# Causal scores packed into 11 PSUM banks per unit instead of 16, cards dealt by bank, and the middle turns as a straight program

## The chip, the cores and the metric

One Trainium2 chip, one core of it. The metric is device microseconds of one execution, the median of several runs. TensorE (PE in the profile) does the matrix products, PEld is its loading of weights, VectorE is DVE, ScalarE is ACT, GpSimd is POOL, and SyncE (SP) issues most transfers. Each engine runs its own program in order and waits on semaphores.

## The reference

Two layers over `x` of shape (8, 512, 256) with a context of shape (8, 512, 128). What matters here is the attention; H = 16 heads of D = 16.

```python
# layer 0
att  = einsum('bhqd,bhkd->bhqk', q, k) * scale            # self attention over 512 tokens
att  = where(causal, att, -inf)
y    = einsum('bhqk,bhkd->bhqd', softmax(att), v)
attc = einsum('bhqd,bhkd->bhqk', qc, kc) * scale          # cross attention with the context
y    = y + einsum('bhqk,bhkd->bhqd', softmax(attc), vc)
x    = x + y @ Wp + bp
x    = x + ffn_with_ternary_weights(layernorm(x))         # 256 -> 1024 -> 256, GELU
# layer 1
x    = x + cross_attention(layernorm(x), ctx) @ Wo + bo   # no mask
x    = x + ffn_with_one_scale_per_tensor(layernorm(x))    # 256 -> 1024 -> 256, GELU
```

## The kernel before, in words

**Units.** The attention is cut into 96 units: 8 batches, three kinds of attention (`x` cross of layer 0, `s` causal self of layer 0, `f` cross of layer 1) and four groups of HU = 4 heads. A *turn* of the program holds 12 units in the order x0 to x3 and s0 to s3 of batch b, then f0 to f3 of batch b - 1. One name, such as s1, stands for the unit of that kind and group in the turn under discussion. `ORDER` is the whole list.

**A unit.** q and k are split into three bf16 parts each, so a product of 96 rows has nearly the precision of f32; these rows lie in a `stack` tile (ring of four), loaded from memory by SP. The unit's work has two halves that are done in different units of time:

- *maxima*: for each tile of 128 queries and each head PE writes scores into a bank of the ring `mx` (2 banks), and DVE reduces each bank to its negated row maxima (`nmax`). Units x and f have 16 banks of 512 columns. Units s already have 11 (`MX_CAUSAL`): the masked part is not computed, so tile 0 of all four heads (4 x 128 columns) shares a bank, tile 1 (256 columns) has two heads in a bank.
- *scores*: POOL splits `nmax` in three bf16 parts (`negmax`), PE turns them (`negmax_T`), ACT copies them to `nrow` and issues a small transfer of 12 KB that writes them as three more rows of the stack. PE then forms the transposed scores, keys on the partitions, with the maximum subtracted, tile j of keys and head c at a time, into a bank of the ring `st` (3 banks); ACT takes the exponential into `probs` (2 slots, one per j); PE multiplies them by the values into `acc` (`values`), ACT copies `acc` to `heads`, PE turns that and DVE divides by the row sums (`heads_out`).

In units s the scores of tile j are 512 - 128 j columns wide: 512, 384, 256 and 128. Before the change each (j, c) has a bank of its own: 16 banks and 16 exponentials. In the diagonal block a product of the identity with a 128 x 128 mask (`mask_st`, `mask_mx`) is added behind each head's product.

**Order.** `unit_slot` writes out the order of a unit's steps. It has 16 *places*, one for each (j, c). At each place stand the scores of that bank; then some banks of the maxima of the unit after next (`third`), dealt evenly by `deal`; at the last place of tile j the `values` of tile j - 1, and at the last place of tile 0 the `values` of the last tile of the unit before with the copy of its `acc`. `negmax` of the next unit stands at place 2, `negmax_T` of the next unit at place 8, which is (j, c) = (2, 0). The transfer that loads the stack of the unit after the next two (`fourth`) is at the unit's beginning. Last come the *cards*, the other work (projections, layer norms, the feed-forward net, residuals), which `slots` deals evenly over the places of several units; `None` is an empty card that keeps a distance.

In a middle turn the cards are: 89 over x0 to s0 (end of layer 1 two batches back, feed-forward net and start of layer 1 of the batch before, the last 17 being the projections fk0, fk1, fq0, fq1 with `settle`, on which the stacks of f0 to f3 depend), 9 over s1 (tokens of the next batch: `load_mid`, `ctx_T`, `stats`, `norm`, `norm_T`), 19 over s2 and s3 (`v` and projections of the next batch's x), 6 and more over f0, and the blend of `ffn_norm` with the projections of the next batch's s over f1 to f3. I write s0.12 for place 12 of unit s0.

**Program.** `walk` writes out turns 0 and 1, then a hardware loop (`eng.Fori`) with five passes for the turns 2 to 6, then turn 7 and the rest. Each engine has its own copy of that loop, so it is left and begun again four times on each. In the loop the semaphores' values are computed from the loop's register (`Count.at`).

The line that ties the loop to 16 places is the choice of bank, `st[n.times(HU * NT).slot(ST_BANKS, k)]`.

Of the kernel before, what the change touches and what calls it, by code (L numbers as in the profile page):

```python
# [36 lines left out]
P = 128  # L37
# [7 lines left out]
HU = 4  # L45
# [36 lines left out]

def exists(u, last):

    return u[0] + (u[1] == "f") <= last


def neighbour(u, k, last=B):

    n = AT[u] + k  # L90
    return ORDER[n] if 0 <= n < len(ORDER) and exists(ORDER[n], last) else None

# [22 lines left out]
def unit_slot(u, others, last, first=False):  # L115
# [10 lines left out]
    for j in range(NT):  # L126
        for c in range(HU):
            out.append(("scores", u, j, c))
            out += maxima[HU * j + c]
            if c == 3 and j:  # L130
                out.append(("values", u, j - 1))
            if (j, c) == (0, 3) and prev:
                out += [("values", prev, NT - 1), ("heads_copy", prev)]
            if (j, c) == (1, 1) and prev:
                out.append(("heads_out", prev))
            if (j, c) == (0, 2) and next_:
                out.append(("negmax", next_))
            if (j, c) == (2, 0) and next_:
                out.append(("negmax_T", next_))
            out += others[HU * j + c]  # L140
# [3 lines left out]
def slots(units, others, last, first=False):  # L144

    out, places = [], NT * HU
    others = deal(others, places * len(units))
    for k, u in enumerate(units):
        out += unit_slot(u, others[places * k:places * k + places], last, first and k == 0)
    return out  # L150
# [141 lines left out]

class Count:
# [23 lines left out]
class Step:  # L317
# [12 lines left out]

    def mx(self, later=0):
# [5 lines left out]
def walk(eng, steps_of):  # L337

    def walk_turn(keys, i):
# [11 lines left out]
def two_layers_kernel(nc, x, ctx_512, L0_xattn_Wk, L0_xattn_bk, L0_xattn_Wq, L0_xattn_bq, L0_xattn_Wv, L0_xattn_bv,  # L351
# [4 lines left out]
    with ExitStack() as ctx:  # L356
# [238 lines left out]
        def st_bank(n, k):  # L595

            return st[n.times(HU * NT).slot(ST_BANKS, k)]
# [5 lines left out]
        def _(sp):  # L603
# [64 lines left out]
            def stack_(s):  # L668
                r, p, g = s.n.slot(STACKS), s.unit[1], s.unit[2]
                if s.n.base >= STACKS:  # L670
                    sp.wait_ge(exp_done, s.n.times(16, ST_BANKS - 16 * (STACKS - 1)).at())
# [214 lines left out]
        def _(act):  # L886
# [38 lines left out]
            def scores(s):  # L925
                (j, c), n = s.args, s.n
                w = T - P * j if s.unit[1] == "s" else T
                if c == 0:
                    act.wait_ge(values_done, n.times(4, VD - P_SLOTS + j + 1).at())
# [599 lines left out]
```

## Time and profile before

| | |
|---|---|
| median of 3 runs | 2048.04 us (2047.91 to 2049.11) |
| profiled execution, its own time | 2049.73 us |
| its span in the trace | 2047.9 us |
| PE / PEld busy | 1735.0 us (85%) / 745.0 us (36%) |
| DVE / ACT / POOL busy | 1348.7 (66%) / 1168.0 (57%) / 739.7 us (36%) |
| mean granted clock of TensorE | 0.911 |

How to read it: PE's busy time counts each matmul from its start to a modelled end, and the matmuls overlap; the time that PE really takes for one is the distance from its start to the start of the next. The granted clock is 1.00 at 2.4 GHz and 0.50 at 1.2 GHz. "Idle before" in a row is time in which the engine did nothing, and behind the arrow stands what ended it; "issue" means that no awaited work is visible.

### The profile page before, as it was taken

What the parts mean: (1) busy time and instruction counts of PE and PEld (TensorE: products, weight loads), DVE (VectorE), ACT (ScalarE), POOL (GpSimd) and SP (SyncE); (2) the same over time, 40 slices, a digit from 0 to 9 for tenths busy, and PEclk for the clock granted to TensorE, in tenths of its full rate; (3) what the DMA queues carried; (4) which work ended last, traced back from release to release, by engine and by line L of the source; (5) the groups of instructions that cost most, each with busy time, mean ns of one, the idle gap of its engine ahead of it and who ended that gap; (6) DMA issues with size and microseconds to landing.
All of it is one profiled execution on the core that took longest, in us unless ns stands there. A gap on an engine that the chain in (4) does not pass through costs nothing.

```text
span 2047.9 us, 34236 instructions
## 1 busy us (share of the span) xinstructions
PE 1735.0 (85%) x10004; PEld 745.0 (36%) x10016; DVE 1348.7 (66%) x2478; ACT 1168.0 (57%) x2178; POOL 739.7 (36%) x984
## 2 busy tenths in 40 slices
PE   5897889987999889987999799987999798777676
PEld 1243334422443244432543244332442243231225
DVE  6567666777667666757677756766677757617378
ACT  1364475566655485556655585557555675552486
POOL 3322525541544126521544136521544042150034
PEclk7798889998999989987999999988999899786898
DMA  7224313232232313331232313222331223005023
GB/s 204 81 77 122 83 32 89 78 90 62 64 104 59 94 48 85 87 81 52 68 100 70 83 48 102 74 77 59 90 87 55 65 56 101 1 26 161 23 81 103
DMA packets 106988, 159.93 MB, mean 78 GB/s; under 512 B 20657, under 2 KB 83249, under 8 KB 106801
## 3 DMA queue, kind: packets, MB, share of 16 engines
q1 hardware_dynamic: 101904, 156.43, 27.7%
q8 instruction: 96, 1.57, 0.3%
q10 hardware_dynamic: 4896, 1.18, 0.3%
q14 instruction: 92, 0.75, 0.1%
HBM read 105.00 MB, written 51.38 MB: 76 GB/s over the span
## 4 chain that ended last, share of the span: by engine, by line
PE 56%; DVE 14%; issue 11%; ACT 8%; POOL 7%; DMA 2%; SPq 1%; ACTq 1%; DVEq 0%; POOLq 0%
PE acc L1390 13%; PE mx L1355 12%; PE st L1376 10%; DVE nmax L1176 8%; PE misc L1330 6%; PE misc L1302 3%; PE misc L1342 3%; PE misc L1417 3%; ACT probs L931 2%; PE misc L1444 2%; POOL qk L823 1%; DMA stack<-parts_fk 1%; POOL parts L825 1%; POOL parts L821 1%; POOL parts L827 1%
## 5 line engine op out<-in xcount | busy, mean ns | idle before, releaser
L1176 DVE TENSOR_REDUCE nmax<-mx 128x1 f32<-128x512 f32 (+2 forms) x1376 | 881.4, 674 | 458.0 <-PE mx L1355 276.7
L931 ACT ACTIVATE probs<-st 128x512 f32<-128x512 f32 (+3 forms) x1536 | 773.7, 548 | 516.1 <-PE st L1376 346.4
L1355 PE MATMUL mx<-stack 96*128 96x512 bf16 (+3 forms) x1536 | 574.3, 385 | 128.7 <-DVE nmax L1176 80.6
L1376 PE MATMUL st<-stack 99*128 99x512 bf16 (+3 forms) x1536 | 565.8, 378 | 68.6 <-ACT probs L931 57.6
L1376 PEld LDWEIGHTS st<-stack 99*128 99x128 bf16 x1536 | 152.0, 100 | 443.9 <-ACT probs L931 262.2
L1355 PEld LDWEIGHTS mx<-stack 96*128 96x128 bf16 x1536 | 154.6, 101 | 342.9 <-DVE nmax L1176 237.4
L821 POOL TENSOR_TENSOR parts<-qk,zero 128x512 bf16<-128x512 f32 x94 | 98.1, 1043 | 302.5 <-ACT qk L914 302.5
L833 POOL TENSOR_TENSOR nparts<-nmax,zero 128x16 bf16<-128x16 f32 x96 | 21.1, 220 | 405.4 <-DVE nmax L1176 398.2
L1390 PE MATMUL acc<-probs,v_x 128*32 128x512 f32 x1024 | 151.0, 665 | 0.0
L1390 PE MATMUL acc<-probs,v_f 128*32 128x512 f32 x1024 | 147.4, 650 | 0.4 <-ACT probs L931 0.3
L1379 PE MATMUL st<-mask_st,identb 128*128 128x128 bf16 x512 | 112.2, 222 | 0.0
L827 POOL TENSOR_TENSOR parts<-qk,parts 128x512 bf16<-128x512 f32 x94 | 108.9, 1158 | 7.4
L823 POOL TENSOR_TENSOR qk<-qk,parts 128x512 f32<-128x512 f32 x94 | 108.7, 1157 | 7.4
L1358 PE MATMUL mx<-mask_mx,identb 128*128 128x128 bf16 x512 | 101.9, 224 | 0.0
L825 POOL TENSOR_TENSOR parts<-qk,zero 128x512 bf16<-128x512 f32 x94 | 97.9, 1042 | 7.4
L1390 PE MATMUL acc<-probs,v_s 128*32 128x512 f32 (+3 forms) x1024 | 97.6, 454 | 0.0
L1330 PE MATMUL misc<-xnT_A,W 128*128 128x512 f32 x192 | 93.2, 608 | 0.0
L859 POOL TENSOR_TENSOR hq<-hid,magic 128x1024 bf16<-128x1024 f32 x32 | 60.6, 1893 | 81.8 <-ACT hid L966 81.8
L938 ACT COPY heads<-acc 128x512 f32<-128x512 f32 x96 | 56.3, 586 | 50.5 <-PE acc L1390 50.3
L890 ACT COPY nrow<-misc 48x128 bf16<-48x128 bf16 x96 | 24.2, 252 | 94.5 <-PE misc L1365 93.7
L1379 PEld LDWEIGHTS st<-mask_st,identb 128*128 128x128 bf16 x512 | 51.1, 100 | 38.2 <-issue 22.3
L1302 PE MATMUL misc<-ident,heads 128*128 128x128 f32 x384 | 61.7, 284 | 3.5 <-ACT heads L938 3.2
(231 smaller groups left out, 2051.5 us busy)
## 6 DMA issues: line engine op xcount, KB each, us to landing
parts_xk<-parts SPq DMA_DIRECT2D x48, 128.0 KB
parts_xq<-parts SPq DMA_DIRECT2D x48, 128.0 KB
stack<-parts_xq SPq DMA_DIRECT2D x32, 192.0 KB, 3.1
stack<-parts_xk SPq DMA_DIRECT2D x32, 192.0 KB, 3.7
parts_sk<-parts SPq DMA_DIRECT2D x48, 128.0 KB
parts_sq<-parts SPq DMA_DIRECT2D x48, 128.0 KB
stack<-parts_sq SPq DMA_DIRECT2D x32, 192.0 KB, 2.9
stack<-parts_sk SPq DMA_DIRECT2D x32, 192.0 KB, 3.5
```

What stands on the lines that cost most here:

```text
L821: pool.tensor_tensor(part[0], qk[:, r, :], zero[:, :].to_broadcast([P, T]), ALU.add).then_inc(qk_split[r], 1)
L823: pool.tensor_tensor(qk[:, r, :], qk[:, r, :], part[0], ALU.subtract).then_inc(qk_split[r], 1)
L825: pool.tensor_tensor(part[1], qk[:, r, :], zero[:, :].to_broadcast([P, T]), ALU.add).then_inc(qk_split[r], 1)
L827: pool.tensor_tensor(part[2], qk[:, r, :], part[1], ALU.subtract).then_inc(qk_split[r], 1)
L931: act.activation(probs[:, j % P_SLOTS, c, T - w:], st_bank(n, 4 * j + c)[:, 0:w], ACT.Exp, scale=SCALE).then_inc(exp_done, 1)
L1176: dve.tensor_reduce(nmax[:, ring, first:first + NT * (len(cs) - 1) + 1:NT], src, AX.X, ALU.max, negate=True).then_inc(mx_free, 1)
L1302: last = pe.transpose(o[:, P * m:P * m + P], t_, id_[:, :])
L1330: last = pe.matmul(misc[misc_slot(s)][:, :], W[w][:, k, P * m:P * m + P], src[:, k, :], start=k == 0, stop=k == ks - 1)
L1355: last = pe.matmul(o, stack[0:ROWS, r, 0, c, P * i:P * i + P], stack[0:ROWS, r, 1, c, 0:w], start=True, stop=not causal)
L1376: last = pe.matmul(o[:, 0:w], stack[0:AUG, r, 1, c, P * j:P * j + P], stack[0:AUG, r, 0, c, T - w:T], start=True, stop=not causal)
L1379: last = pe.matmul(o[:, 0:P], identb[:, :], mask_st[:, :], start=False, stop=True)
L1390: last = pe.matmul(acc[32 * c:32 * c + 32, T - w:T], v_aug[p][:, j, HU * g + c, :], probs[:, j % P_SLOTS, c, T - w:T], start=j == 0, stop= ...
```

## The change

- `ST_CAUSAL` gives the scores of a causal unit 11 banks: tiles 0 and 1 four banks each of one head, tile 2 two banks of two heads (2 x 256 columns), tile 3 one bank of four heads (4 x 128). PE fills a bank with one wait and one signal, ACT takes it with one exponential.
- Where a head's share of the bank is exactly 128 columns (tile 3 of the scores, tile 0 of the maxima), the mask is written first, as one product 512 columns wide whose moving operand repeats the 128 columns of the mask four times; the heads' products are added to it.
- A causal unit has 11 places instead of 16, and maxima and cards are dealt over those. So x0 to s0 have 75 places instead of 80, s1 11 instead of 16, and s2 with s3 22 instead of 32. `negmax_T` moves to place 8 of 11, which is again the first bank of tile 2.
- The hardware loop is gone: all turns are written out, and all semaphore values are constants. The bank ring's position is counted by `ST_BEFORE`.

```diff
+ST_FULL = [(j, [c], T) for j in range(NT) for c in range(HU)]
+ST_CAUSAL = [(j, [c], T - P * j) for j in (0, 1) for c in range(HU)] + [(2, [c, c + 1], 2 * P) for c in (0, 2)] + \
+    [(3, [0, 1, 2, 3], P)]
...
 def unit_slot(u, others, last, first=False):
-    maxima = deal([("maxima", third, k) for k in banks_of(third)] if third else [], NT * HU)
+    banks = scores_in(u)
+    maxima = deal([("maxima", third, k) for k in banks_of(third)] if third else [], len(banks))
...
+    for k, (j, cs, w) in enumerate(banks):
+        nth = k - min(m for m, bank in enumerate(banks) if bank[0] == j)
+        ends = k == last_of_tile(u, j)
+        out.append(("scores", u, k))
+        out += maxima[k]
+        if ends and j:
+            out.append(("values", u, j - 1))
+        if ends and j == 0 and prev:
+            out += [("values", prev, NT - 1), ("heads_copy", prev)]
+        if (j, nth) == (1, 1) and prev:
+            out.append(("heads_out", prev))
+        if (j, nth) == (0, 2) and next_:
+            out.append(("negmax", next_))
+        if (j, nth) == (2, 0) and next_:
+            out.append(("negmax_T", next_))
+        out += others[k]
...
 def walk(eng, steps_of):
-    walk_turn(TURNS[0], None)
-    with eng.Fori(0, B - 3) as i:
-        walk_turn(TURNS[1], i)
-    walk_turn(TURNS[-1], None)
+    for keys in TURNS:
         for key in keys:
             if key[0] in steps_of:
-                steps_of[key[0]](Step(key, i))
+                steps_of[key[0]](Step(key, None))
...
             def scores(s):      # ACT
-                act.wait_ge(st_full, n.times(16, 4 * j + c + 1).at())
-                act.activation(probs[:, j % P_SLOTS, c, T - w:], st_bank(n, 4 * j + c)[:, 0:w], ACT.Exp, scale=SCALE).then_inc(exp_done, 1)
+                act.wait_ge(st_full, n.at(k + 1))
+                act.activation(probs[:, j % P_SLOTS, cs[0]:cs[-1] + 1, T - w:],
+                               st_bank(n, k)[:, 0:len(cs) * w].rearrange("p (c w) -> p c w", w=w),
+                               ACT.Exp, scale=SCALE).then_inc(exp_done, 1)
...
             def scores(s):      # PE; maxima in the same manner
-                last = pe.matmul(o[:, 0:w], stack[0:AUG, r, 1, c, P * j:P * j + P], stack[0:AUG, r, 0, c, T - w:T],
-                                 start=True, stop=not causal)
-                if causal:
-                    last = pe.matmul(o[:, 0:P], identb[:, :], mask_st[:, :], start=False, stop=True)
+                whole = causal and w == P
+                if whole:
+                    pe.matmul(o[:, :], identb[:, :], mask_st[:, :].unsqueeze(1).to_broadcast([P, len(cs), P]), start=True, stop=False)
+                for c in cs:
+                    own = o[:, (c - cs[0]) * w:(c - cs[0]) * w + w]
+                    last = pe.matmul(own, stack[0:AUG, r, 1, c, P * j:P * j + P], stack[0:AUG, r, 0, c, T - w:T],
+                                     start=not whole, stop=c == cs[-1] if whole else not causal)
+                    if causal and not whole:
+                        last = pe.matmul(own[:, 0:P], identb[:, :], mask_st[:, :], start=False, stop=True)
```

## Rows read from the trace of the kernel before

**Rows 1.** The page: busy time of each engine
```profile
PE 1735.0 (85%) x10004; PEld 745.0 (36%) x10016; DVE 1348.7 (66%) x2478; ACT 1168.0 (57%) x2178; POOL 739.7 (36%) x984
```

**Rows 2.** Windows of turns 2, 3, 6, f3's copy to next; busy, clock, DMA
```profile
454.74:682.25 227.51, 201.13 (x1188) 86.28 (x1188) 152.97 (x294) 134.76 (x262) 87.47 (x118) 0.95 0.29 78
682.25:910.92 228.67, 202.58 (x1188) 86.38 (x1188) 153.13 (x294) 134.56 (x262) 87.48 (x118) 0.94 0.28 76
...
1368.06:1592.64 224.58, 201.00 (x1188) 86.45 (x1188) 152.83 (x294) 134.54 (x262) 87.51 (x118) 0.95 0.28 75
```

**Rows 3.** Timeline of PE where turn 4 begins
```profile
902.35 1.07 PE L1390 MATMUL acc<-probs,v_f 128*32 128x512 f32 x8
905.77 0.39 PE L1376 MATMUL st<-stack 99*128 99x512 bf16 x1 [2.35 <-issue]
```

**Rows 4.** Waits: engine line, waited for; us in total, times, longest
```profile
PE st L1376 <- issue: 10.6, 4, 3.0
PE mx L1355 <- DMA stack<-parts_fk: 26.4, 8, 9.0
```

**Rows 5.** Timeline of PE at s2.0 of turns 3 and 4
```profile
797.00 0.39 PE L1355 MATMUL mx<-stack 96*128 96x512 bf16 x1 [2.57 <-DMA stack<-parts_fk]
...
1027.80 0.39 PE L1355 MATMUL mx<-stack 96*128 96x512 bf16 x1 [2.17 <-DMA stack<-parts_fk]
```

**Rows 6.** Windows, copy of s0's acc to that of s1's, turns 3 and 4
```profile
783.70:803.08 19.38, 15.86 (x117) 9.28 (x116) 12.68 (x31) 8.56 (x23) 5.64 (x13) 0.91 0.58 148
1014.92:1032.20 17.28, 14.17 (x117) 8.14 (x116) 12.59 (x31) 8.57 (x23) 5.66 (x13) 1.00 0.62 164
```

**Rows 7.** Timelines of POOL and SP: fk0's first split, loading f0's stack
```profile
767.11 1.04 POOL L821 TENSOR_TENSOR parts<-qk,zero 128x512 bf16<-128x512 f32 x1 [5.08 <-ACT qk L914]
...
792.10 1.35 SPq L678 DMA_DIRECT2D stack<-parts_fk  x3
```

**Rows 8.** Windows, acc copy to acc copy, of x2, x3, s0 and s2, turn 3
```profile
731.66:750.38 18.72, 16.22 (x134) 8.40 (x133) 8.96 (x18) 16.20 (x26) 8.39 (x8) 1.00 0.28 65
750.38:768.18 17.80, 17.58 (x129) 9.61 (x128) 12.27 (x30) 12.09 (x24) 4.68 (x4) 1.00 0.20 46
768.18:783.70 15.52, 14.82 (x113) 7.51 (x112) 7.25 (x13) 8.53 (x22) 14.52 (x17) 1.00 0.18 56
...
803.08:818.65 15.57, 14.97 (x94) 6.30 (x93) 10.85 (x19) 8.49 (x21) 9.89 (x13) 1.00 0.11 32
```

**Rows 9.** Timelines of PE and ACT from negmax_T in s0 of turn 7
```profile
1698.28 0.22 PE L1365 MATMUL misc<-identb,nparts 128*48 128x128 bf16 x1 [0.61 <-POOL nparts L839]
1698.88 0.73 ACTq L922 DMA_DIRECT2D stack<-nrow  x1
...
1702.74 0.39 PE L1376 MATMUL st<-stack 99*128 99x512 bf16 x1
```

**Rows 10.** DMA issues: KB each, median us from issue to landing
```profile
stack<-parts_xk SPq DMA_DIRECT2D x32, 64.0 KB, 3.7
x_later<-y_s SPq DMA_DIRECT2D x1, 512.0 KB, 2.6
```

**Rows 11.** Timeline of PE in s2's last tile
```profile
811.18 0.22 PE L1376 MATMUL st<-stack 99*128 99x128 bf16 x1
811.24 0.22 PE L1379 MATMUL st<-mask_st,identb 128*128 128x128 bf16 x1
811.30 0.38 PE L1355 MATMUL mx<-stack 96*128 96x512 bf16 x1
811.52 0.22 PE L1376 MATMUL st<-stack 99*128 99x128 bf16 x1
```

**Rows 12.** Groups by line and shape: busy us, mean ns of one, idle before
```profile
L1176 DVE TENSOR_REDUCE nmax<-mx 128x1 f32<-128x512 f32 x1152 | 749.9, 686 | 324.0 <-PE mx L1355 276.7 <-PE mx L1358 39.5 <-POOL nparts L837 1.8
L931 ACT ACTIVATE probs<-st 128x512 f32<-128x512 f32 x1152 | 642.2, 602 | 429.9 <-PE st L1376 346.4 <-PE st L1379 78.0 <-ACT nrow L890 1.6
L931 ACT ACTIVATE probs<-st 128x128 f32<-128x128 f32 x128 | 31.1, 278 | 26.3 <-PE st L1379 25.0
```

More of the change, by code:

```diff
@@ L91, in neighbour, with scores_in, last_of_tile @@
     return ORDER[n] if 0 <= n < len(ORDER) and exists(ORDER[n], last) else None
+def scores_in(u):
+    return ST_CAUSAL if u[1] == "s" else ST_FULL
+def last_of_tile(u, j):
+    return max(k for k, bank in enumerate(scores_in(u)) if bank[0] == j)
 def banks_in(u):
@@ L122, in unit_slot @@
     next_, third, fourth = (neighbour(u, k, last) for k in (1, 2, 3))
-    maxima = deal([("maxima", third, k) for k in banks_of(third)] if third else [], NT * HU)
+    banks = scores_in(u)
+    maxima = deal([("maxima", third, k) for k in banks_of(third)] if third else [], len(banks))
     if fourth:
         out.append(("stack", fourth))
[L126 to L140, printed above, removed]
+    for k, (j, cs, w) in enumerate(banks):
[14 more added lines that the diff above has]
+        out += others[k]
     return out
 def slots(units, others, last, first=False):
-    out, places = [], NT * HU
-    others = deal(others, places * len(units))
+    out, places = [], [len(scores_in(u)) for u in units]
+    others = deal(others, sum(places))
     for k, u in enumerate(units):
-        out += unit_slot(u, others[places * k:places * k + places], last, first and k == 0)
+        done = sum(places[:k])
+        out += unit_slot(u, others[done:done + places[k]], last, first and k == 0)
     return out
@@ L290 @@
     MX_BEFORE.append(MX_BEFORE[-1] + len(banks_in(u)))
+ST_BEFORE = [0]
+for u in ORDER:
+    ST_BEFORE.append(ST_BEFORE[-1] + len(scores_in(u)))
 class Count:
@@ L329, in ring, with st @@
         return Count(START[key or self.key][r], RING_PER_TURN[r], self.i)
+    def st(self, later=0):
+        return Count(ST_BEFORE[AT[self.unit] + later], 0, None)
     def mx(self, later=0):
@@ L595, in st_bank @@
         def st_bank(n, k):
-            return st[n.times(HU * NT).slot(ST_BANKS, k)]
+            return st[n.slot(ST_BANKS, k)]
         block = ctx.enter_context(nc.Block())
@@ L670, in stack_ @@
                 if s.n.base >= STACKS:
-                    sp.wait_ge(exp_done, s.n.times(16, ST_BANKS - 16 * (STACKS - 1)).at())
+                    sp.wait_ge(exp_done, s.st(1 - STACKS).at(ST_BANKS))
                 for w, name in enumerate("qk"):
@@ L1387, in values @@
                     pe.wait_ge(heads_full, n.at(1))
-                pe.wait_ge(exp_done, n.times(16, 4 * j + 4 + ST_BANKS).at())
+                pe.wait_ge(exp_done, s.st().at(last_of_tile(s.unit, j) + 1 + ST_BANKS))
                 for c in range(HU):
```

35 lines of the change are left out of this document (19 added, 16 removed).

## The prediction

> **What bounds the kernel now.** I read the page first, then the windows turn by turn and unit by unit, then the waits, then the timelines at the places they named. PE is busy 85% of the span, DVE 66%, ACT 57%, POOL 36% [rows 1]. The windows of single units show what that average hides: in x3 and s0 PE is busy 17.58 of 17.80 and 14.82 of 15.52 us, so these units last as long as PE's instructions. In x2 it is busy 16.22 of 18.72, and ACT with 16.20 is as loaded as PE [rows 8]. In s2 DVE has 10.85 of 15.57 us, ACT 8.49: ACT bounds no causal unit.
>
> So the question for each part is which of PE's instructions or idle times it changes. Two idle times stand out.
>
> First, the loop's ends. PE's first scores of turn 4 come 2.35 us after the modelled end of its last work, and the releaser is "issue" [rows 3]. The list of waits has exactly four of these at that line, 10.6 us in all [rows 4], and the loop of five passes starts anew four times. The turns show what one costs with all that hangs on it. Turn 3 lasts 228.67 us, and turns 4 and 5 repeat it within 0.3; each begins behind a restart and has one in its last unit. Turn 6, after which the loop is only left, has none in its last unit and lasts 224.58: 4.1 us less. Turn 2 has one at its end but is entered, not restarted: 227.51, 1.15 us less [rows 2]. This second part I read as what a stall leaves behind it, mainly a slower clock.
>
> Second, at s2.0 PE starts the maxima of f0 and waits for f0's stack, 2.57 us in turn 3 and 2.17 in turn 4 [rows 5]; eight such waits make 26.4 us, the longest of 9.0 in the last part, which the change leaves alone [rows 4]. That leaves 17.4 us in turns 1 to 7. It costs more than the wait: s1's window lasts 19.38 us in turn 3 at a clock of 0.91, and 17.28 in turn 4 at 1.00 [rows 6]. Less the 0.40 by which the waits differ, 1.7 us are the clock. I found 0.91 in five of the seven turns.
>
> **The change part by part.**
>
> *No loop.* It removes four restarts at 4.1 + 1.15 = 5.25 us: 21.0 us. Turns 0, 1 and 7 are straight program already and show no wait of this kind (four in all, all at restarts), so nothing is expected in its place. For waits on constants instead of computed values I give nothing: inside the loop too PE's products follow each other at 0.06 and 0.22 us [rows 11], which is their streaming. On what a restart costs, the Trainium skill has two rules. "Runtime: NRT & Kernel Launch", in "Instruction fetch mechanics", says that a taken branch to a page outside the small window makes the engine fetch before it goes on; the idle time of 2.35 us agrees in kind. "Advanced Engine Details and Errata", in "Control Flow Timing", gives a compare-and-branch 108 ns: by that alone, an estimate, four restarts were worth 0.4 us and the term of 21.0 would be gone.
>
> *Fewer exponentials.* Two heads of tile 2 and all four of tile 3 share one. For tile 3 ACT saves 4 x 278 - 602 = 510 ns [rows 12], some 0.8 us in a unit with tile 2, 27 us over 32 units. All of it lies under PE's work (ACT is idle for 7 us in s2) and brings nothing; without that cover it would bring those 27.
>
> *Wide masks.* PE takes 0.06 us from one product of 128 columns to the next, and 0.22 for 512 columns [rows 11]. Before, four heads cost 8 x 0.06 = 0.48 us; after, 0.22 + 4 x 0.06 = 0.46. Columns set the time, not the number of products. Two such banks in 32 units: 0 to -2.6 us; I take 0. That a repeated operand is read slower no row shows; bound: the mask as dear as four separate ones, +1 us.
>
> *Cards by bank, x0 to s0.* 89 cards on 75 places in place of 80. Card 72 (counting from 0), fk0, falls on place 75 x 73 / 89, that is x3.13; before it was s0.1. It gains four places of x3 and s0, at (17.80 + 15.52) / 32 = 1.04 us each [rows 8]; without their share of cards I take 3.2 us. fk0's split begins at 767.11, f0's stack is issued until 793.45, PE goes on at 797.00 [rows 5, 7]: a chain of 29.9 us that POOL and SP set, while PE reaches the place after 27.3. With 3.2 more, PE arrives after 30.5, later than the stack. fq1 moves from s0.12 to s0.7 and remains ahead of POOL. So the waits vanish, but for a rest of the longest: 16.8 of the 17.4. Since the distance ends only 0.6 us on the good side, I take 15; bounds 8 and 17. The slow clock after them: 5 x 1.7 = 8.5, of which I take 7; bounds 0 and 9.
>
> *The same, feed-forward net.* Its steps stand 6% closer together. x2 gains `down_T` and `down` of the third tile, s0 loses projections. Work moves from units that PE fills into one that ACT nearly fills [rows 8]. PE's time is the same; its waits for ACT and POOL in x0 to x2 may grow by the distance lost, up to 1 us a turn. I take +2 in all; bounds -3 and +7.
>
> *Maxima in s2 and s3.* 16 banks on 11 places instead of 16: one or two at a place. DVE needs 16 x 0.686 = 11.0 us for them [rows 12] and PE has only two banks. Before, tile 3 was the tight spot (0.34 us of PE for each place [rows 11] against 0.69 of DVE); after, tiles 0 and 1 are, with 11 maxima, while tiles 2 and 3 have 5. Both orders lose about 1.2 us a unit by my count: 0, bounds -8 and +8 over 16 units.
>
> *negmax_T nearer to the next unit.* This is the new wait. In turn 7's s0 PE takes 4.46 us from negmax_T to the next unit's first scores [rows 9], with seven score places, five banks of maxima and 0.5 of waiting for DVE on the way. After the change two places (384 columns or 0.16 us less) and two banks of maxima (3 x 0.27 less) are left: 4.46 - 0.16 - 0.8 - 0.5 = 3.0, and I take 2.9 for s0, 3.0 for s3; with the norm's transposes in between 3.75 in s1, with a projection 3.95 in s2. In that time ACT must copy and the transfer must land, and all later PE work is queued behind that wait, DVE and ACT behind PE. The issue comes 0.60 us after negmax_T; landing is not shown. Above: in turn 7 scores began 3.86 us after the issue, without idle time before them [rows 9], so at most 3.86. Below: nothing is issued faster than its own 0.73. Rows beside it: 64 KB into the stack land after 3.7, the fastest row after 2.6 [rows 10]. With so small a transfer I take 2.6: the chain is 3.2, and waits are 0.3 in s0 and 0.2 in s3, 0.5 x 8 turns = +4 us. At 3.86 the chain is 4.46, waits 1.6, 1.5, 0.7, 0.5, 4.3 a turn: +34. At best 0. "DMA: Bandwidth & Descriptors", section "Anatomy of one DMA — SWDGE (gpsimd) path", in the Trainium skill has a fixed cost of about 2.0 us; as an estimate from it the chain is 2.6 us and this term 0.
>
> **Sum.** -21 - 15 - 7 + 2 + 0 + 4 = -37 us. Against the profiled execution's 2049.7 us (span 2047.9, 1.8 around it) that is 2012.7; its own time is 1.7 above the median, so against 2048.0 it is **2011 us**, 1.8% less.
>
> **Rivals.**
>
> *A: only the loop pays.* f0's stack is late all the same, because the chain starts when PE reaches fk0, and denser cards delay PE before it. For: the new slack is 0.6 us only. Against: s0 has fewer cards ahead of s1. Then -21 + 2 + 4 = -15: 2033.
>
> *B: slower.* The transfer of `nrow` at the end of each causal unit takes the place of the waits removed. The other terms are -41 together, 5.1 us a turn. With a chain of t us the waits are (t - 2.9) + (t - 3.0) + (t - 3.75) + (t - 3.95), which is 5.1 at t = 4.7, a landing of 4.1 us. At t = 5.0 it is 6.4 a turn, +51: 2058. For: in s1 the DMA engines are 58% busy and move 148 GB/s [rows 6], and 64 KB took 3.7. Against: 3.86 sufficed in turn 7.
>
> *C: the restart is cheap* and the four idle times belong to the turn's first step. Then 21 less gain: 2032. Against: the entry and the exit of the loop carry the same step without it. The 108 ns that the Trainium skill gives for a branch would mean this.
>
> *D: better still.* Sparser maxima and free DVE take the 8 us, negmax_T costs nothing, 17 and 9 are full: 2048 - 21 - 17 - 9 - 8 - 3 = 1990.
>
> **Chances and range.** Forecast 0.64, A 0.16, B 0.08 (half of it slower than before), C 0.04, D 0.08. The range of 1994 to 2034 leaves out D's end, B and a part of A: the low end is the sum with -17, -9, -3, no negmax wait and half of the 8; the high end is A, or the forecast with a landing of 3.3 us. About 0.2% (4 us) is what a measurement tells from no change: faster by more 0.91, within 0.03, slower by more 0.06.
>
> **What would show it.** No "issue" waits of PE at the scores; turns 2 to 6 alike, at 217 to 220 us where they were 228. At s2.0 no wait for stack<-parts_fk above 1 us in turns 1 to 6 and clock 1.00 in s1; else the step of four places is wrong. Idle time before the first scores of s1 and f0 below 0.5 us; above 1.5, B. Exponentials 32 x 5 fewer with s units no shorter for it. What would make the forecast wrong most: a landing above 3.2 us, or a POOL that reaches fk0 late.

## The result and the profile after

The changed kernel takes 2037.16 us (median of 4 runs, 2036.70 to 2038.55), the kernel before beside it 2048.57 us (4 runs): a ratio of 0.9943 with a 95% interval of 0.9925 to 0.9960. It is faster, by 11.4 us and not by the 37 us forecast: the direction was right, the size was not, and the time lies outside the range of 1994 to 2034. The profiled run has a span of 2035.1 us where it was 2047.9.

The page's first lines, after; the counts of PE's products and ACT's exponentials fell as computed, busy times hardly [rows 1]:

```profile
span 2035.1 us, 28512 instructions
...
PE 1716.1 (84%) x9812; PEld 722.3 (35%) x9824; DVE 1343.8 (66%) x2478; ACT 1154.5 (57%) x2018; POOL 742.2 (36%) x984
```

The list of PE's waits, after:

```profile
PE mx L1382 <- DVE nmax L1199: 107.3, 155, 5.3
...
PE mx L1382 <- DMA stack<-parts_fk: 17.8, 5, 9.0
...
PE st L1408 <- DMA stack<-nrow: 4.1, 5, 1.1
```

The four waits for "issue" at the scores [rows 4] are gone. The wait for the first feed-forward net's stack fell from 26.4 to 17.8 us. The wait for `nrow` came at the size expected. The first line is the one that the prediction never asked for. In the trace of before it reads:

```profile
PE mx L1355 <- DVE nmax L1176: 80.6, 122, 5.1
```

PE waits 26.7 us more for DVE's maxima, in 33 more places. The windows (start to end, length, then busy time of PE, PEld, DVE, ACT and POOL, clock, DMA share, GB/s) say where the time went. After, turns 2, 3 and 6, then x0, x2, x3, s0, s1 (also of turn 4), s2 and s3 of turn 3, and s1 of turn 0:

```profile
465.77:689.54 223.77, 200.58 (x1164) 83.41 (x1164) 151.99 (x294) 133.16 (x243) 87.62 (x118) 0.94 0.29 77
689.54:911.75 222.21, 198.19 (x1164) 83.35 (x1164) 152.14 (x294) 132.93 (x242) 87.62 (x118) 0.95 0.28 77
1355.17:1577.21 222.04, 197.20 (x1164) 83.15 (x1164) 151.87 (x294) 133.04 (x242) 87.62 (x118) 0.96 0.29 77
...
689.54:716.92 27.38, 22.19 (x103) 8.96 (x103) 19.08 (x39) 10.73 (x20) 2.13 (x6) 0.88 0.50 136
...
740.95:760.11 19.16, 17.00 (x142) 9.16 (x141) 9.39 (x17) 15.99 (x27) 8.42 (x12) 1.00 0.24 62
760.11:779.12 19.01, 17.79 (x117) 8.88 (x116) 12.65 (x31) 12.05 (x23) 9.10 (x9) 1.00 0.02 5
779.12:793.50 14.38, 14.38 (x109) 7.26 (x108) 7.30 (x13) 8.15 (x16) 13.36 (x18) 1.00 0.48 139
793.50:808.19 14.69, 12.81 (x102) 7.05 (x101) 11.79 (x31) 7.54 (x16) 2.42 (x8) 1.00 0.64 171
1015.59:1030.77 15.18, 12.95 (x102) 7.01 (x101) 11.73 (x31) 7.62 (x17) 2.49 (x8) 1.00 0.64 166
808.19:824.11 15.92, 14.67 (x91) 6.13 (x92) 10.72 (x19) 8.40 (x17) 10.01 (x10) 1.00 0.12 35
824.11:837.09 12.98, 12.53 (x82) 4.93 (x81) 10.02 (x18) 7.25 (x15) 10.35 (x16) 1.00 0.48 134
...
160.12:188.35 28.23, 15.66 (x102) 6.40 (x101) 15.93 (x23) 8.51 (x15) 2.58 (x7) 0.75 0.47 136
```

A middle turn lasts 222 to 224 us where 217 to 220 was forecast. In turn 3 s1 stands at a clock of 1.00 and at 14.69 us (it was 19.38, [rows 6]), s2 is 0.35 us longer and s3 0.2 shorter, x3 is 1.2 us longer and s0 as much shorter [rows 8]. Two windows are far longer than before. Their rows of before, x0 of turns 2 and 3 and s1 of turn 0, are:

```profile
454.74:477.98 23.24, 19.85 (x101) 8.37 (x101) 18.44 (x38) 10.84 (x21) 2.13 (x6) 1.00 0.58 160
682.25:706.49 24.24, 21.10 (x101) 8.56 (x101) 18.62 (x38) 10.84 (x20) 2.12 (x6) 0.93 0.52 135
...
161.98:181.51 19.53, 13.58 (x112) 6.72 (x111) 13.93 (x21) 8.55 (x21) 2.65 (x10) 0.83 0.58 164
```

x0 takes 27.0 to 27.4 us in every middle turn and in turn 7, where it took 23.2 to 24.3 (26.0 in turn 4); s1 of turn 0 takes 28.2 instead of 19.5. Summed over turns 2 to 6 (acc copy to acc copy, before to after, in us): x0 121.9 to 136.4, x1 126.8 to 121.6, x2 93.6 to 96.1, x3 89.0 to 95.1, s0 77.6 to 71.7, s1 94.1 to 75.6, s2 and s3 143.9 to 144.4, f0 to f2 291.8 to 286.9, f3 99.3 to 83.6. Turns 0 and 1 together are 11 us longer.

The timelines of DVE and PE in x0 of turn 3 show why. Before, DVE:

```profile
694.41 1.89 DVE L1176 TENSOR_REDUCE nmax<-mx 128x1 f32<-128x512 f32 x3
696.22 1.37 DVE L1093 TENSOR_SCALAR xn_C<-x,mv_E,rstd_E 128x256 f32<-128x256 f32 x4
```

After, DVE:

```profile
700.54 1.40 DVE L1104 BATCH_NORM_STATS2 stats_E<-x 128x6 f32<-128x256 f32 x4
701.85 0.41 DVE L1108 BATCH_NORM_AGGREGATE mv_E<-stats_E 128x2 f32<-128x6 f32 x4
702.18 1.26 DVE L1199 TENSOR_REDUCE nmax<-mx 128x1 f32<-128x512 f32 x2
703.85 1.38 DVE L1116 TENSOR_SCALAR xn_C<-x,mv_E,rstd_E 128x256 f32<-128x256 f32 x4 [0.41 <-POOL rstd_E L805]
```

and PE, which needs the banks that DVE empties behind that:

```profile
702.90 0.39 PE L1382 MATMUL mx<-stack 96*128 96x512 bf16 x1 [0.51 <-DVE nmax L1199]
...
705.89 0.39 PE L1382 MATMUL mx<-stack 96*128 96x512 bf16 x1 [1.78 <-DVE nmax L1199]
...
707.81 0.61 PE L1382 MATMUL mx<-stack 96*128 96x512 bf16 x1 [1.31 <-DVE nmax L1199]
```

Between the statistics and the norm stood three sets of maxima before (one set is DVE's reduction of one bank) and stand two now: by the denser dealing `norm` and `finish` moved from places x0.12 and x0.13 to x0.11 and x0.12, while `stats` stayed at x0.9. So DVE reaches the norm before POOL has `rstd` and waits 0.41 us, and what follows is all on DVE, four norms, 1.38 us together, and a peak of 1.2, with fewer maxima between. The clock over the window fell to 0.88.

### The profile page after: what moved, and what is told of

Same layout as the page of the kernel before. It is cut to its first block, busy times and chain, and to the rows that moved or that the text cites. A ratio compares the mean times of both kernels' runs of the same rounds, so it can differ in the third digit from the quotient of the medians.

```text
span 2035.1 us, 28512 instructions
## 1 busy us (share of the span) xinstructions
PE 1716.1 (84%) x9812; PEld 722.3 (35%) x9824; DVE 1343.8 (66%) x2478; ACT 1154.5 (57%) x2018; POOL 742.2 (36%) x984
## 4 chain that ended last, share of the span: by engine, by line
PE 52%; DVE 21%; ACT 10%; issue 7%; POOL 7%; DMA 2%; SPq 1%; ACTq 0%; POOLq 0%; DVEq 0%
PE acc L1422 13%; DVE nmax L1199 11%; PE mx L1382 11%; PE st L1408 9%; PE misc L1353 6%; PE misc L1325 3%; PE misc L1365 3%; PE misc L1449 3%; ACT probs L952 2%; DVE hid L1153 1%; PE misc L1476 1%; ACT hid L976 1%; POOL parts L848 1%; POOL qk L844 1%; ACT hqT L911 1%
## 5 line engine op out<-in xcount | busy, mean ns | idle before, releaser
L952 ACT ACTIVATE probs<-st 128x512 f32<-128x512 f32 (+1 forms) x1376 | 759.4, 591 | 523.2 <-PE st L1408 374.4
L1382 PE MATMUL mx<-stack 96*128 96x512 bf16 (+3 forms) x1536 | 550.9, 380 | 142.4 <-DVE nmax L1199 107.3
L1408 PE MATMUL st<-stack 99*128 99x512 bf16 (+3 forms) x1536 | 538.1, 372 | 53.6 <-ACT probs L952 48.9
L1382 PEld LDWEIGHTS mx<-stack 96*128 96x128 bf16 x1536 | 147.9, 99 | 382.1 <-DVE nmax L1199 281.0
L1422 PE MATMUL acc<-probs,v_x 128*32 128x512 f32 x1024 | 155.5, 683 | 0.0
L1411 PE MATMUL st<-mask_st,identb 128*128 128x128 bf16 x384 | 82.3, 222 | 0.0
L1385 PE MATMUL mx<-mask_mx,identb 128*128 128x128 bf16 x384 | 82.2, 222 | 0.0
L911 ACT COPY nrow<-misc 48x128 bf16<-48x128 bf16 x96 | 24.3, 253 | 89.8 <-PE misc L1392 89.5
```

The lines of the kernel that those rows point to most:

```text
L952: act.activation(probs[:, j % P_SLOTS, cs[0]:cs[-1] + 1, T - w:], st_bank(n, k)[:, 0:len(cs) * w].rearrange("p (c w) -> p c w", w=w), ACT. ...
L1382: last = pe.matmul(own, stack[0:ROWS, r, 0, c, P * i:P * i + P], stack[0:ROWS, r, 1, c, 0:w], start=not whole, stop=c == cs[-1] if whole e ...
L1408: last = pe.matmul(own, stack[0:AUG, r, 1, c, P * j:P * j + P], stack[0:AUG, r, 0, c, T - w:T], start=not whole, stop=c == cs[-1] if whole ...
L1411: last = pe.matmul(own[:, 0:P], identb[:, :], mask_st[:, :], start=False, stop=True)
L1422: last = pe.matmul(acc[32 * c:32 * c + 32, T - w:T], v_aug[p][:, j, HU * g + c, :], probs[:, j % P_SLOTS, c, T - w:T], start=j == 0, stop= ...
```

## The experiments

Every kernel was timed beside the kernel before; kernels of one group ran on one chip. One kernel, run in two groups, gave ratios of 0.9768 and 0.9817 with intervals that just miss each other. So ratios are held against each other within a group; across groups the windows of the traces decide. The changed kernel itself is in none of the groups; its ratio is that of the result. The first group tells the parts apart.

**Straight program alone.** The kernel before with

```diff
-    walk_turn(TURNS[0], None)
-    with eng.Fori(0, B - 3) as i:
-        walk_turn(TURNS[1], i)
-    walk_turn(TURNS[-1], None)
+    for keys in TURNS: ...
```

> The kernel before with one edit: the seven turns are written out, and the scores keep their 16 places a unit, one mask per head. Theory (the loop's restart was worth what the prediction gave it, and the new idle time in x0 to s0 belongs to the new dealing): four times 4.1 us in f3 and 1.15 us behind it go, 21 us in all, so 2026 to 2030 us; x0 of turns 2 to 6 stays at 23 to 24.5 us. Rival (the straight program itself pushes the lost time into x0, because TensorE no longer gives the other engines a pause at each turn): x0 rises to 26 us or more and the time is 2037 us or above.

Measured: 2029.2 us, ratio 0.9905 (0.9883 to 0.9928), span 2025.4. The theory holds; x0 of turns 2 to 6 is 24.1 to 24.4 us. This one edit is worth 19.5 us by the ratio (22.7 between the medians, 22.5 between the spans), more than the whole change.

**Banks and wide masks, old places.** The changed kernel, with the 16 places of `unit_slot` kept; the scores of a bank stand where their first head stood.

> The changed kernel (scores in 11 banks, wide masks, straight program), with the cards dealt over 16 places a unit as before. Theory (banks and wide masks are worth nothing by themselves, since the sum of columns is the same): within 3 us of the kernel that only has its loop written out, so 2025 to 2031 us, faster than the full change; x0 at 23 to 24.5 us, the waits for the first feed-forward net's stack back in eight places with some 26 us. Rival (fewer matmuls and exponentials do pay): 2020 us or less. Second rival (11 large banks need their buffers back sooner than 16 places deal them out): a new wait at the scores and 2033 us or more.

Measured: 2039.65 us, ratio 0.9949 (0.9935 to 0.9964): 10 us slower than the straight program with 16 banks. The time is the second rival's, its cause is not: PE waits at the scores as long as before (57.0 and 57.2 us). The waits for f0's stack are back (28.5 us in 8), and x0 of turns 2 to 6 is at 23.4 to 24.2 us, as expected. What grew is PE's wait for DVE's maxima. First the straight program with 16 banks, then this kernel:

```profile
PE mx L1351 <- DVE nmax L1172: 82.7, 136, 5.7
```

```profile
PE mx L1381 <- DVE nmax L1198: 95.1, 158, 5.7
```

PE's timeline in s3 shows how, four banks of maxima behind each other where scores of one head each used to stand between:

```profile
830.50 0.39 PE L1407 MATMUL st<-stack 99*128 99x128 bf16 x4
830.72 0.60 PE L1381 MATMUL mx<-stack 96*128 96x512 bf16 x2
831.89 0.39 PE L1381 MATMUL mx<-stack 96*128 96x512 bf16 x1 [0.57 <-DVE nmax L1198]
832.48 0.39 PE L1381 MATMUL mx<-stack 96*128 96x512 bf16 x1 [0.21 <-DVE nmax L1198]
```

s2 and s3 together are 0.8 us longer in turns 1 to 6, 1.6 in turn 7 and 1.9 in turn 0: 8 of the 16.6 us by which the spans differ. Of the rest f2 has 3.9 and x1 3.4 us, units whose granted clock differs from turn to turn in either kernel; and this profiled execution was 4.2 us above its median, the other 2.0 below. In this kernel five of the 16 places have no scores, so it shows what 11 banks cost when the places stay, not what they cost on 11 places: in the changed kernel s2 and s3 are 28.9 us together in each of turns 2 to 6, in the straight program 28.8 to 28.9.

**One more card in x0.** The changed kernel with

```diff
-("stats", b, "E"), None, None, ("norm", b, "E"),
+("stats", b, "E"), None, None, None, ("norm", b, "E"),
```

> The changed kernel with one more empty card between the statistics and the normalization of the second half in x0, so that three sets of maxima stand between them as before, and not two. Theory (x0 lost 3 to 4 us a turn because DVE waits there for POOL's rstd, the next set of maxima stands behind that wait, and TensorE waits for its mask): x0 of turns 2 to 7 falls from 27.3 to 23.3 to 24.5 us, six times 3 to 4 us, so 2013 to 2020 us. Rival (x0 is long because more maxima stand on DVE in each place, or because the clock is low there for a cause further ahead): x0 stays above 26 us and the time within 4 us of 2037.

Measured: 2023.8 us, ratio 0.9868 (0.9842 to 0.9894). The window of x0 in turn 3, and the timeline of DVE in it:

```profile
687.93:710.89 22.96, 19.56 (x101) 8.17 (x101) 17.59 (x37) 10.72 (x20) 2.13 (x6) 1.00 0.59 161
```

```profile
698.92 1.40 DVE L1104 BATCH_NORM_STATS2 stats_E<-x 128x6 f32<-128x256 f32 x4
...
700.56 1.85 DVE L1199 TENSOR_REDUCE nmax<-mx 128x1 f32<-128x512 f32 x3
702.33 1.37 DVE L1116 TENSOR_SCALAR xn_C<-x,mv_E,rstd_E 128x256 f32<-128x256 f32 x4
```

Three sets of maxima stand between again, DVE doesn't wait, and the clock is 1.00. x0 of turns 2 to 6 sums to 119.3 us instead of 136.4, turn 7's is 4.3 shorter; x1 and x2 behind it take 7.0 of that back. PE's wait for maxima falls from 107.3 to 90.9 us. One empty card is worth some 12 to 15 us (spans 2022.8 against 2035.1; 0.9868 against 0.9943, the latter from another group). In x0 itself it is worth more than the idle time it removes: in turn 3 PE waited 3.60 us in the three rows above and 0.51 + 1.28 us in the same stretch here, and the window is 4.4 us shorter. The other 2.6 us are PE's busy time, 22.19 against 19.56 for nearly the same products: the clock, 0.88 and 1.00. The theory holds, though the time lies above the 2013 to 2020 us expected.

**The peak of the weights behind the negated maxima.** In turn 0 the changed kernel has `w_peak` of the third weight at s1.1, ahead of `negmax` of s2 at s1.2, where it was behind it. One `None` puts it behind again.

> The changed kernel with one empty card in turn 0 ahead of the weights' peaks, so that the peak with the all-reduce on POOL stands behind the unit's negated maxima again, as before the change. Theory (s1 of turn 0 lost 8.7 us because the negated maxima of s2 stand on POOL behind the all-reduce): s1 of turn 0 falls from 28.2 us to 19 to 21 us, and the time to 2028 to 2032 us; if turn 1 waits for the weights anyway, part of it comes back there and 2034 is left. Rival (the all-reduce delays whatever stands behind it, and here the same amount is lost at another place): 2036 to 2038 us.

Measured: 2039.9 us, ratio 0.9943 (0.9924 to 0.9961): a miss, and the rival's side. s1 of turn 0 fell only to 24.9 us, and s2 behind it and x0 of turn 1 took 2.3 and 2.1 us of that back. The negated maxima do stand right again: POOL splits them at 164.3 us (162.5 before, 175.7 after the change), and PE's wait of 3.1 us for them is gone. DVE's timelines say what I had overlooked. Before, after, and in this kernel (each fence one kernel):

```profile
161.87 2.28 DVE L1035 TENSOR_REDUCE wsum<-hid 128x1 f32<-128x2048 f32 x1
164.07 1.14 DVE L1176 TENSOR_REDUCE nmax<-mx 128x2 f32<-128x512 f32 x2
...
169.98 0.15 DVE L1045 TENSOR_SCALAR wscale<-wtot 128x1 f32<-128x1 f32 x1 [4.14 <-POOL wtot L774]
```

```profile
159.16 2.27 DVE L1058 TENSOR_REDUCE wsum<-hid 128x1 f32<-128x2048 f32 x1
161.35 1.14 DVE L1199 TENSOR_REDUCE nmax<-mx 128x2 f32<-128x512 f32 x2
167.51 0.15 DVE L1068 TENSOR_SCALAR wscale<-wtot 128x1 f32<-128x1 f32 x1 [5.01 <-POOL wtot L795]
```

```profile
171.81 0.15 DVE L1068 TENSOR_SCALAR wscale<-wtot 128x1 f32<-128x1 f32 x1 [5.52 <-POOL wtot L795]
```

`w_scale` stood three places behind `w_peak` and stands two behind it in both changed kernels. DVE waits there for POOL's all-reduce, with all maxima behind it, 5.5 us instead of 4.1. Moving the peak alone left that distance short. In s1 of turn 0 PE still waits 8.3 us for maxima (5.9 before), and 2.1 for `nrow`, which is new; how much of this that one distance makes, no run separates.

The second group restores the other distances.

**Old places at the start.** The changed kernel with the card in x0, and in which the causal units of turn 0 and s0 of turn 1 have 16 places again, with 11 banks:

```diff
+def places_of(u):
+    if u[1] != "s" or u[0] == 0 or u == (1, "s", 0):
+        starts = {(j, cs[0]): k for k, (j, cs, w) in enumerate(scores_in(u))}
+        return [(j, c, starts.get((j, c))) for j in range(NT) for c in range(HU)]
```

> The changed kernel with the extra card in x0, and in turn 0 and x0 to s0 of turn 1 the cards and maxima again dealt over 16 places a causal unit (its scores stay in 11 banks). In the trace of the changed kernel these stretches together lost 10 to 11 us. Theory (they lost it to the denser dealing, in the profiled old dealing the same stretches lasted 9.5 us less): a ratio to the kernel before of 0.9868 - 9.5 / 2048 = 0.982, 2009 to 2015 us. Rival (the weights' preparation sets the length of these turns, and what is won in one unit is lost in the next, as with the card ahead of the peak): within 3 us of the kernel with the extra card, a ratio of 0.986 to 0.988.

Measured: 2016.22 us, ratio 0.9831 (0.9807 to 0.9855). s1 of turn 0 is back at 19.4 us, x2 of turn 1 at 18.4 (24.3 after the change, 18.4 before). Against the kernel with the card in x0 turn 0 is 9.4 us shorter and turn 1 another 1.0: there x1 and x2 gave 7.7, and s0 and s1 took 5.0. The theory holds in sum by the windows, which give 10.4 us. By the time it is less: the kernel with masks per head, the closest to a base in this group, stands at 0.9859, so 6 us, and the two intervals overlap a little.

**norm_T a place later.** The kernel with the card in x0, and in `layer1_norm`

```diff
-("norm", b, "C"), None, ("norm_T", b, "C"), None]
+("norm", b, "C"), None, None, ("norm_T", b, "C")]
```

> The changed kernel with the extra card in x0, and the transposes of the norm of layer 1 one place further behind the norm in x3. Theory (x3 lost 1.2 us a turn because TensorE waits there for DVE's norm): x3 of turns 2 to 7 falls from 19.0 to 17.8 us, 7 us in all with turn 1's waits left as they are, a ratio of 0.983 to 0.984. Rival (the work is late on DVE for all that stands behind, and the wait turns up at the next product): x3 stays at 19.0, or x3 and s0 together lose nothing, a ratio of 0.986 to 0.988.

Measured: 2016.27 us, ratio 0.9832 (0.9810 to 0.9854). x3 of turns 2 to 7 is 18.05 to 18.13 us where it was 19.01, and PE's wait of 1.2 us for the norm is gone from it. The theory holds, with 5.7 us in x3 where 7 were expected.

**Masks per head.** The kernel with the card in x0, and `whole = False` in both places.

> The changed kernel with the extra card in x0 and the masks of banks of four heads as four products of 128 columns again. Theory (columns set TensorE's time, 0.46 against 0.48 us a bank): the same within 2 us of the kernel with the extra card, a ratio of 0.985 to 0.989; s2 and s3 of the middle turns within 0.1 us. Rival (the wide mask pays because TensorE has six instructions less to take in a unit, or costs because its operand repeats): 4 us or more either way, s3 at 13.2 us or at 12.7.

Measured: 2024.34 us, ratio 0.9859 (0.9836 to 0.9883), s2 and s3 of the middle turns 15.93 and 13.00 against 15.91 and 12.98. The card in x0 with wide masks gave a span of 2022.8, this one 2020.9. Wide masks are worth nothing that can be told, in either direction.

**All three distances.**

> The changed kernel with the extra card in x0, the transposes of layer 1's norm one place later, and the old places in turn 0 and x0 to s0 of turn 1. Theory (the three losses lie in different stretches and add up): 0.9868 less 9.5 and 7 us, a ratio of 0.979, 2002 to 2009 us. Rival (TensorE then reaches the same transfers earlier and waits there, above all at the first feed-forward net's stack): a ratio of 0.982 or more, with waits for that stack in turns 2 to 6 above 1 us.

Measured: 2005.68 us, ratio 0.9768 (0.9745 to 0.9791). The gains add up by the windows: turns 0 and 1 last 459.1 us together (459.3 with the old places alone, 464.3 with the later norm_T alone), x3 of turns 2 to 7 108.4 (114.1 and 108.4). That makes 5 to 6 us more than either alone. The ratio gives 13 against 0.9831 and 0.9832, of which some must be chance: the same kernel in the third group has 0.9817, and the span is only 2 us below the other two (the profiled execution is the slowest of its five). No new wait for f0's stack appears (17.4 us in 4, as 17.8 in 5 after the change).

The third group asks what the banks are for, once the distances are right.

**Sixteen banks, cards moved.** The straight program of the first experiment, with the two card edits and

```diff
-layer1_end(b - 2) + ffn_main(b - 1) + layer1_start(b - 1)
+layer1_end(b - 2) + ffn_main(b - 1) + layer1_start(b - 1) + [None] * 6
```

> The kernel before as straight program, with its 16 banks, 16 exponentials and masks per head, in which only the cards are moved: the extra card between statistics and normalization in x0, norm_T of layer 1 a place later, and six empty cards behind the projections, so that from turn 2 on every card of x0 to x3 and the projections in s0 stand where the best version so far has them. Theory (of the change only the straight program and the cards' earlier places pay, the 11 banks bring nothing): within 4 us of that version, a ratio of 0.975 to 0.979, 2000 to 2008 us. Rival (the 11 banks do bring something once the cards stand right, by shorter s0 and s1): 6 us or more above it. Second rival (the kernel with 11 banks and old places was 10 us slower than the one with 16, so the banks cost): 5 us or more below it.

**The same with the loop kept.**

> The kernel before with its loop and its 16 banks, in which only the cards of the middle turns are moved as in e9_sixteen_banks. Theory (loop and cards are independent): slower than e9_sixteen_banks by the same 20 to 23 us that the straight program gained alone, so a ratio of 0.985 to 0.989, and faster than the full change without touching banks or program. Rival (the idle time of a restart gives the other engines time that the denser cards then don't need): less than 15 us slower than e9_sixteen_banks.

**The best version again, and with negmax_T a place earlier.**

> The same kernel as e8_both, for a comparison on the same chip with the others of this call: 0.977 again, 2001 to 2009 us. If the theory of the clock is right (f2 lasts 17.3, 18.6, 18.9 or 20.1 us in one and the same order of instructions), its f2 units differ between the turns and from the run before, and no wait does.

> The best version so far (extra card in x0, norm_T later, old places at the start) with negmax_T of the next unit at place 7 of 11 in the causal units, the last bank of tile 1, in place of 8. Theory (TensorE's 6 us of waits for the transfer of nrow, in six places, are what the later turning costs): they go, s1 of the middle turns 0.4 to 1 us shorter, 3 to 6 us in all, a ratio of 0.974 to 0.975. Rival (the waits only move the next wait, DVE's maxima or POOL's nparts): within 2 us, and a new wait for POOL's nparts at negmax_T.

Measured, all on one chip, against the kernel before with 2049.17 us:

| kernel | us | ratio | interval |
|---|---|---|---|
| 11 banks, three distances (e11) | 2010.91 | 0.9817 | 0.9796 to 0.9838 |
| the same, negmax_T earlier (e10) | 2007.87 | 0.9803 | 0.9779 to 0.9826 |
| 16 banks, straight, cards moved (e9) | 2003.65 | 0.9766 | 0.9741 to 0.9791 |
| 16 banks, loop kept, cards moved (e12) | 2018.81 | 0.9848 | 0.9829 to 0.9866 |

- The best version was expected at 0.977 again and came out at 0.9817, above its range: a miss.
- The 11 banks bring nothing: with 16 the kernel is 7 us faster (spans 2001.2 and 2006.5), the second rival's side. It is the fastest of all, 2.3% below the kernel before. The cause is not the one seen with the old places. PE does wait 84.5 us for maxima with 16 banks and 92.5 with 11, but 4.6 of these 8 us lie in s2 of turns 2 to 6, and there s2 and s3 sum to 144.5 us in both. Shorter with 16 banks are s1 of turns 2 to 7, by 5.2 us (3.9 less of waits for `nrow`, 3.3 less for f0's stack), x3 of the same turns by 3.7, and turns 0 and 1 by 3.8; f2 of turns 2 to 6 is 4.5 longer, with its clock. From turn 1's s1 on the causal units have 16 places in the one kernel and 11 in the other, so this pair does not tell banks from places.
- The loop costs 15 to 17 us with the new cards too: a little less than the 19.5 alone, whose interval of 4.6 us to either side covers it, and between theory and rival. f3 of turns 2 to 5 is 20.6 to 21.6 us again, 18.3 more in all than in the straight program, and f0 and f1 of turns 2 to 6 have 1.6 more. The x0 that follows a restart lasts 23.3 to 24.0 us and not 24.05, 2.1 less in four turns, but the x1 behind it takes 2.1 back (24.3 to 25.3 us against 24.46): a restart gives nothing back. What makes the difference smaller is f2 of turns 2 to 6, 4.7 us shorter with its clock.
- Moving cards in the loop's text, with no change to banks or program, gives 2018.81 us, 31 below the kernel before and, across groups, 18 below the full change.
- The earlier turning cuts the waits for `nrow` from 5.0 to 1.6 us, and the wait for f0's stack rises from 16.7 to 19.3. The intervals overlap and the spans are within 0.4 us: nothing that can be told, the rival.

## Why the prediction was right and wrong

**No loop, -21.** Right: 19.5 us measured alone, spans 22.5 apart. f3 of turns 2 to 5 became 15.8 us shorter in the changed kernel, where 4 x 4.1 = 16.4 was the term. The second part, 1.15 us of slower clock behind each restart, is not borne out: in the straight program x0 of turns 3 to 6 still takes 24.1 to 24.4 us at 0.93, as behind most restarts (24.1 to 24.3; 26.0 in turn 4). What took its place is 1.6 us in f0 and f1, and in the trace 5.6 in f2, whose clock differs from turn to turn in any kernel. So 17 us are shown in the units, and that the time met the term so well is partly luck. f0 and f1 fell from 20.86 and 17.50 to 20.77 and 17.28 us in every middle turn, 0.3 us a turn that goes with the loop (and returns with it in e12). Waits on computed values are the likely cause; no run separates them. They were priced at nothing. The 108 ns of the Trainium skill ("Advanced Engine Details and Errata", "Control Flow Timing") are far below the 4 us that a restart costs here with all that hangs on it; rival C is out.

**Fewer exponentials and wide masks, 0.** Right for the masks, tested alone (the repeated operand, bounded at +1, costs nothing that can be told). In the trace a bank costs PE what was computed:

```profile
801.23 0.38 PE L1405 MATMUL st<-mask_st,identb 128*128 128x512 bf16 x1
801.45 0.39 PE L1408 MATMUL st<-stack 99*128 99x128 bf16 x4
801.67 0.38 PE L1382 MATMUL mx<-stack 96*128 96x512 bf16 x1
```

0.22 us for the mask and 0.22 for four heads, as computed from [rows 11]. The packing as a whole was priced at nothing. It brings no gain in any run, and in two pairs of kernels the one with 11 banks is slower, by 10 us with equal places and by 7 with 11 places against 16, and the difference lies in other units each time. What it costs on 11 places by itself stays open.

**Cards by bank, f0's stack, -15 and -7.** Right in the middle turns: their five waits fell from 11.8 to 0.8 us, and s1 of turn 4, at 17.28 with a wait of 2.17 [rows 5, 6], is 15.18, the wait less. The clock in s1 of these turns is 1.00. s1 of turns 1 to 7 became 19.3 us shorter (18.5 of it in turns 2 to 6), where the two terms have 22. Outside the middle turns the waits rose, by 1.4 us in turn 1 (to 3.15, where none above 1 us was forecast) and 1.0 in turn 7, so that the list shows 8.6 less and not 15. In e2, with the old places, they are all back: it is the places that did it. Rival A is out.

**Maxima in s2 and s3, 0.** Right: +0.1 us a turn, s2 0.3 longer and s3 0.2 shorter.

**negmax_T nearer, +4.** The sum was right, 4.1 us of waits in five places, and the places were wrong. I had put them behind s0 and s3; all five are at the end of s1 of turns 2 to 6, as in turn 3 (ACT's timeline, then PE's):

```profile
799.29 0.76 ACTq L943 DMA_DIRECT2D stack<-nrow  x1
```

```profile
803.04 0.39 PE L1408 MATMUL st<-stack 99*128 99x512 bf16 x1 [0.36 <-DMA stack<-nrow]
```

That is 3.75 us from issue to landing; in the other four turns it is 4.0 to 4.5. Behind s3 a weight load of PE that waited for the same transfer started 2.67 us after the issue, behind s0 2.2 to 2.3. So 2.6 us was right for s3 and low for s1, where the 16 DMA engines were busy for 0.95 of that time:

```profile
799.29:803.04 3.75, 3.39 (x34) 1.66 (x31) 2.06 (x4) 2.17 (x4) 0.12 (x1) 1.00 0.95 235
```

One value for all units could not be right, and the sum of 4 us was met by luck. Rival B, which wanted more than 4.1 us of landing everywhere, is out. The fixed 2.0 us that the prediction sets beside this is, by the heading it quotes, for transfers through GpSimd; ACT issues these, and with it the term would have been 0.

**The same, feed-forward net, +2 (-3 to +7).** This is the step that failed. I costed the 6% by which all cards move together as a small loss of distance, "up to 1 us a turn". Instead the dealing rounds: the places from statistics to norm went from three to two, and with that went a set of maxima that covered POOL's `rstd`. In the trace x0 became 14.5 us longer over turns 2 to 6 and 3.9 in turn 7, x3 6.1 (partly by the projections that moved into it: s0 became 5.9 shorter), x2 2.5; x1 became 5.2 shorter. x0 to s0 came out 12.0 us longer in turns 2 to 6, and 16.6 above the forecast, which had 4.6 less for the restarts. Measured, then, this term is +12 to +17 us and not +2. And the term looked at x0 to s0 of the middle turns alone. Turns 0 and 1, where causal units carry the preparation of the weights, were in no term: 52 cards on 33 places instead of 48 went with 5.3 us more in turn 0, and 59 places instead of 64 in x1 to s0 with 5.7 more in turn 1, 11 us in all. With these two corrections the sum is -37 + 14.6 + 11 = -11.4, which meets the measured -11.4 more closely than its parts deserve (turn 7's x0, for one, is not in it). The experiments show the term directly: the card alone takes 12.3 us off the span, and three restored distances bring the ratio from 0.9943 to 0.9768 or 0.9817, 26 to 36 us (spans 2035.1 to 2012.3 and 2006.5).

The range missed because this term stands in it at +2: its high end, 2034, is rival A or a slower landing, and even its own bound was only +7. (A landing of 3.3 us, which the prediction gives as the other way to 2034, makes waits of 16 us by its own formula, so 2023.) What pointed to more was in the list of waits for DVE, where 80.6 us in 122 places said that DVE's order, not its 66%, is what PE waits for most.

## What to carry to other kernels

When a list of work is dealt over fewer places, don't scale distances: write out old and new place of every producer and consumer, and look for each pair that lost a whole place, in the first and the last turns too. A pair on an engine that works in order costs all that stands behind it, here a 0.4 us wait of DVE that became 3 to 4 us of x0, 1.4 of which the units behind it took back. And time each part of a joint change alone: here the straight program and earlier cards paid, the packing did not, and an empty card was worth more than 192 matmuls and 160 exponentials less. Before a difference between turns becomes a price, compare them unit by unit and set aside the units whose clock changes by itself: the 1.15 us for what a restart leaves behind came mostly from one of those.

## What the hardware showed beyond that

**One order of instructions, several lengths.** f2 has the same instructions in every middle turn and lasts 17.3, 18.6, 18.9 or 20.1 us, with the granted clock. The windows of f2 in turns 2 and 3 of the kernel with all three distances, and in turn 2 of the one with the card in x0:

```profile
642.29:662.41 20.12, 17.49 (x74) 5.16 (x73) 14.06 (x24) 10.23 (x20) 7.98 (x8) 0.83 0.09 28
863.39:881.98 18.59, 15.97 (x74) 4.83 (x73) 13.87 (x24) 10.01 (x20) 7.97 (x8) 0.91 0.10 31
```

```profile
653.93:671.20 17.27, 14.56 (x74) 4.65 (x73) 13.69 (x24) 10.01 (x19) 7.97 (x8) 1.00 0.12 33
```

All three have the same 74 matmuls, and DVE, ACT and POOL do nearly the same work (DVE 14.06, 13.87 and 13.69 us); it is the clock that differs, 0.83, 0.91 and 1.00. The same kernel run again (e11) had 18.6, 18.6, 18.7, 18.6 and 20.0 where e8 had 20.1, 18.6, 18.9, 18.9 and 18.7. As an estimate, five such units that go from 18.6 to 20.1 us each move a run by 8 us, which is in keeping with the spread of 2000.6 to 2014.1 us in the five runs of e8. What decides which clock a turn gets I can't say.

**An all-reduce on POOL costs far more than its row.** POOL's timeline in turn 0, after:

```profile
108.25 0.41 POOL L795 PARTITION_ALL_REDUCE wtot<-wsum  x1 [10.79 <-DVE wsum L1058]
...
159.93 1.16 POOL L848 TENSOR_TENSOR parts<-qk,parts 128x512 bf16<-128x512 f32 x1
167.10 0.38 POOL L795 PARTITION_ALL_REDUCE wtot<-wsum  x1 [6.02 <-issue]
175.72 0.20 POOL L854 TENSOR_TENSOR nparts<-nmax,zero 128x16 bf16<-128x16 f32 x1 [8.25 <-issue]
```

Its own row says 0.38 us. At the second one shown DVE had its input ready at 161.4, POOL was done with other work at 161.1, the result came at 167.5, and POOL's next instruction, which waited for nothing that the profile shows, started at 175.7. So POOL was taken for 14.6 us. The trace has a MODIFY_POOL_CONFIG of this line at 161.3 us, as POOL's other work ends, and one of the next instruction's line at 167.4, as the all-reduce ends: the two long gaps stand behind these. That the 6 us ahead of the row do not follow from the input the first one shows: there the MODIFY_POOL_CONFIG was at 97.6, POOL had been idle for 10.8 us, and the result came 0.5 us after the input (108.1 to 108.7). At all four all-reduces of the weights POOL's next instruction starts 7.5 to 8.6 us after the row's start (at one of them DVE's maxima came late too). The Trainium skill ("Perfetto Trace Analysis", "GPSIMD Engine Instruction") says that such spans aren't to be trusted and that one goes by the distance between starts; the trace agrees, with 0.38 us beside 8.62 from start to start.
